# Transposing the experts' down products: fp32r products of 256 tokens, gate weights spread over the partitions by DMA, a lag of seven steps

## What is computed

```python
scores = softmax(x @ gate_w)                       # x: tokens x 128, gate_w: 128 x 8
topk_w, topk_idx = top_k(scores, 2)
topk_w = topk_w / (sum(topk_w) + 1e-20)
w_per_expert = einsum('nke,nk->ne', one_hot(topk_idx), topk_w)
for e in range(8):
    hid = silu(x @ w_gate[e]) * (x @ w_up[e])      # tokens x 256
    y = y + w_per_expert[:, e:e+1] * (hid @ w_down[e])
shared = silu(x @ ws_gate) * (x @ ws_up) @ ws_down
return x_residual + y + shared
```

## Time and profile before

| | us |
|---|---|
| median of 3 runs | 204.69 (204.68 to 205.4) |
| profiled execution | 204.75 |
| its span | 202.9 |
| TensorE busy | 191.8 (95%) |
| VectorE busy | 156.5 (77%) |
| ScalarE busy | 137.6 (68%) |
| GpSimd busy | 96.7 (48%) |

### The profile page before, as it was taken

How to read it: one execution, slowest core, us unless ns; L and a number is a source line. 1 busy time by engine, 2 the same in 40 slices (tenths; PEclk the granted TensorE clock), 3 DMA queues, 4 the chain that set the end, 5 groups by cost and what they waited for, 6 DMA issues and landing times.

```text
span 202.9 us, 4609 instructions
## 1 busy us (share of the span) xinstructions
PE 191.8 (95%) x1626; PEld 151.3 (75%) x1626; DVE 156.5 (77%) x418; ACT 137.6 (68%) x318; POOL 96.7 (48%) x145
## 2 busy tenths in 40 slices
PE   7999999899999779988999999999989999999995
PEld 7788787767877566755575657576668799999994
DVE  2579999668768695779989999999973866458744
ACT  2499878679767767289989898987976232452220
POOL 7599217688467757707739992003300017500430
PEclk9999999999999999999999999999999999999999
DMA  6980407703552015689632400000000000000001
GB/s 173 384 208 3 155 2 227 243 2 54 74 74 37 2 39 115 73 102 117 94 88 83 76 2 0 5 0 3 0 0 3 5 0 0 3 0 13 3 1 38
DMA packets 13301, 12.69 MB, mean 63 GB/s; under 512 B 1072, under 2 KB 11312, under 8 KB 13280
## 3 DMA queue, kind: packets, MB, share of 16 engines
q1 hardware_dynamic: 12176, 11.15, 25.8%
q10 hardware_dynamic: 1008, 1.06, 1.6%
q0 software_dynamic: 96, 0.20, 0.7%
HBM read 10.96 MB, written 1.44 MB: 61 GB/s over the span
## 4 chain that ended last, share of the span: by engine, by line
PE 71%; DVE 14%; ACT 8%; issue 5%; POOL 1%; DVEq 0%; ACTq 0%; POOLq 0%
PE ps L990 13%; PE ps L949 10%; PE ps L1014 8%; PE ps L926 6%; PE ps L875 6%; PE ps L759 6%; PE ps L908 5%; ACT prob L635 4%; PE ps L891 4%; PE ps L847 3%; DVE q_t L1220 3%; PE ps L731 3%; DVE low L1210 3%; PE ps L772 3%; DVE prob_t L1283 2%
## 5 line engine op out<-in xcount | busy, mean ns | idle before, releaser
L1220 DVE CUSTOM_DVE_ANT_0 q_t<-ps,mask_add 128x512 f32<-128x512 f32 x64 | 41.4, 685 | 3.4 <-PE ps L908 2.1
L509 POOL TENSOR_TENSOR prob<-prob,rec 128x512 f32<-128x512 f32 x32 | 32.7, 1047 | 22.8 <-DVE rec L1279 22.8
L635 ACT ACTIVATE prob<-ps,low 128x256 f32<-128x256 f32 x64 | 29.5, 487 | 7.4 <-DVE low L1210 7.4
L669 ACT ACTIVATE q_t<-q_t,low 128x512 f32<-128x512 f32 x44 | 29.4, 718 | 4.3 <-DVE low L1220 4.1
L949 PEld LDWEIGHTS ps<-ident,q_t 128*128 128x128 f32 x176 | 19.5, 141 | 9.4 <-ACT q_t L669 3.2
L949 PE MATMUL ps<-ident,q_t 128*128 128x128 f32 x176 | 24.1, 277 | 2.4 <-ACT place_k L712 0.8
L548 POOL TENSOR_TENSOR place_k<-place_k 128x256 f32<-128x256 f32 x10 | 7.3, 733 | 38.7 <-DVE place_k L1245 38.7
L1210 DVE TENSOR_REDUCE low<-ps 128x2 f32<-128x512 f32 x32 | 20.4, 683 | 5.9 <-PE ps L847 5.8
L655 ACT ACTIVATE q_t<-ps 128x512 f32<-128x512 f32 x18 | 10.6, 599 | 21.0 <-PE ps L990 21.0
L1266 DVE TENSOR_TENSOR q_t<-q_t,ps 128x512 f32<-128x512 f32 x18 | 12.2, 684 | 11.4 <-PE ps L990 8.2
L875 PE MATMUL ps<-prob_t,v 128*64 128x256 f32 x128 | 17.3, 390 | 2.3 <-DVE prob_t L1283 2.0
(11 more groups left out here) (183 smaller groups left out, 471.9 us busy)
## 6 DMA issues: line engine op xcount, KB each, us to landing
k_stack<-k_dram SPq DMA_DIRECT2D x18, 128.0 KB
wg<-in_L_ffn_w_gate SPq DMA_DIRECT2D x1, 1024.0 KB, 5.4
wu<-in_L_ffn_w_up SPq DMA_DIRECT2D x1, 1024.0 KB, 7.9
q_stack<-q_dram SPq DMA_DIRECT2D x6, 144.0 KB
k_dram<-prob SPq DMA_DIRECT2D x1, 768.0 KB, 3.6
w_in<-in_L_attn_Wq ACTq DMA_DIRECT2D x2, 256.0 KB, 5.4
context<-in_ctx SPq DMA_DIRECT2D x1, 512.0 KB, 5.7
w_in<-in_L_attn_Wv SPq DMA_DIRECT2D x1, 512.0 KB, 7.4
```

The lines of the kernel that those rows point to most:

```text
L509: nc.gpsimd.tensor_tensor(pr, pr, rec1[:, s % 2, r, :].unsqueeze(2).to_broadcast([P, C, S]), ALU.mult).then_inc(s_norm1, 1)
L635: e = nc.scalar.activation(prob1[:, s % 3, r, c * S:(c + 1) * S], ps[:, 2 * (s % 2) + r, c * S:(c + 1) * S], ACT.Exp, bias=low1[:, s % 2, ...
L669: nc.scalar.activation(prob2[n % 3][:, c, :], score2[n % 2][:, c, :], ACT.Exp, bias=low2[:, n % 2, c:c + 1], scale=-1.0).then_inc(s_exp2, 1)
L1220: nc.vector.tensor_tensor_reduce(out=score2[n % 2][:, c, :], in0=ps[:, 2 * (n % 2) + c, :], in1=mask_add[:, c, :], scale=1.0, scalar=3e38, ...
```

## The change

- Down products are transposed: down weights stationary, 256 tokens moving, as three fp32r products for each half f. A step has 6 products of 256 columns (L1070 of the changed kernel). y then lies with features on the partitions and tokens along the columns, so the output is written as (D, B, S); the host only views it transposed.
- The down weights are split in high and low parts on GpSimd (`split_down`), 8 in cross-attention steps n = 23 to 30 and one after row 1's normalising.
- The hidden values are split as well. VectorE writes the product silu x up back into the up bank, ScalarE copies it from there as the high part (`high_of_hidden`, one silu later), and VectorE subtracts for the low part (L1331). `s_hid` is now raised by that subtraction. There are 3 up banks (2, 3 and 6) and 8 buffers of hidden parts.
- The gate weight of a token now belongs to a column. `w_e` goes to DRAM and comes back spread over the 128 partitions (`w_wide`: 128 x 2048 floats a row, [token][expert]); VectorE multiplies by every 8th of them (`wide_weight`).
- The lag is 7 steps. In row 1 the shared expert comes last. Row 0 is summed by GpSimd wholly; in row 1 GpSimd adds for k = 1 and 2, VectorE for k = 3 to 7 (L1320) and in the end (L1304). The residual x2 is added on TensorE by two products with the identity (L1066), in steps j = 0 and 17.
- The gate weights are cut in two parts of 8 and 12 instructions. Row 0's come at n = 33, around the last copy of transposed probabilities; row 1's in steps 10 and 11, and its exponential in step 9 instead of 8.

```diff
-LAG_D = 2
-BY_POOL = 5
+LAG_D = 7
+HIDS = LAG_D + 1
+U_BANKS = (2, 3, O_BANK)
+BY_POOL = 2
...
-    6: [("turn2", 1, 0), ("turned2", 1, 0)],
-    7: [("gate", 1, 0)],
-    8: [("shift", 1, 0), ("gate_exp", 1, 0)],
-    11: [("weights", 1, 0)],
+    7: [("turn2", 1, 0), ("turned2", 1, 0)],
+    8: [("gate", 1, 0)],
+    9: [("shift", 1, 0), ("gate_exp", 1, 0)],
+    10: [("weights", 1, 0)],
+    11: [("weights", 1, 1)],
...
+            for b in range(B):
+                sp.wait_ge(s_we, b + 1)
+                load(w_dram[b].rearrange("(c p) e -> p c e", p=P), w_e[:, b * C:(b + 1) * C, :], d_wdram)
+                sp.wait_ge(d_wdram, 16 * (b + 1))
+                sp.wait_ge(s_low2, C * N_CROSS)
+                load(w_wide[:, b, :], w_dram[b].rearrange("(o t) e -> o (t e)", o=1).to_broadcast([P, S * NE]), d_wwide[b])
...
+            def split_down(k):
...
+                split(wd[:, (k - 1) % (NE + 1), :, :], [wd_parts[k][:, i, :, :] for i in range(2)]
+                      ).then_inc(s_wdparts, 1)
...
+            def high_of_hidden(i):
+
+                act.wait_ge(s_prod, i + 1)
...
+                nc.scalar.copy(hid[i % HIDS][:, 0, :, :], ps[:, U_BANKS[i % 3], :].rearrange("p (f t) -> p f t", f=FC)
+                               ).then_inc(s_hidhi, 1)
...
             def silu_step(i):
                 act.wait_ge(s_g, i + 1)
                 if i >= 2:
-                    act.wait_ge(s_hid, i - 1)
+                    act.wait_ge(s_prod, i - 1)
                 nc.scalar.activation(silu[i % 2], ps[:, i % 2, :], ACT.Silu).then_inc(s_silu, 1)
+                if i >= 1:
+                    high_of_hidden(i - 1)
...
                     up(i % 2, 0).then_inc(s_g, 1)
-                    if i >= 2:
-                        pe.wait_ge(s_hid, i - 1)
-                    up(2 + i % 2, 1).then_inc(s_u, 1)
+                    if i >= 3:
+                        pe.wait_ge(s_hid, i - 2)
...
+                    up(U_BANKS[i % 3], 1).then_inc(s_u, 1)
...
+                    if e == NE:
+                        pe.wait_ge(s_x2, b + 1)
+                        for c in range(C):
+                            mm(ps[:, y_bank(j), c * P:(c + 1) * P], x2[:, b * C + c, :], ident[:, :],
+                               start=c == 0, stop=False)
+                    for f in range(FC):
+                        for part, (hi, wi) in enumerate(BIG_PARTS):
+                            last = mm(ps[:, y_bank(j), 0:S], w[:, wi, f, :], hid[j % HIDS][:, hi, f, :],
+                                      start=e != NE and f == 0 and part == 0,
+                                      stop=f == FC - 1 and part == len(BIG_PARTS) - 1)
+                    last.then_inc(s_y, 1)
...
+            def outputs(j):
...
+                if b or k >= 3:
+                    dve.wait_ge(s_acc, b * NE + (min(k - 2, BY_POOL) if b else k - 2))
+                v.tensor_tensor(y_part[k % 2], y, wide_weight(b, e), ALU.mult).then_inc(s_ypart, 1)
+                if b and k > BY_POOL:
+                    dve.wait_ge(s_ypart, j + 1)
+                    if k == BY_POOL + 1:
+                        dve.wait_ge(s_acc, NE + BY_POOL)
...
+                    v.tensor_tensor(acc[:, b, :], acc[:, b, :], y_part[k % 2], ALU.add).then_inc(s_sum, 1)
...
             def hidden_step(i):
                 if i < N_FFN:
...
-                    v.tensor_tensor(hid[i % 3], silu[i % 2].rearrange("p (f t) -> p f t", f=FC),
-                                    ps[:, 2 + i % 2, :].rearrange("p (f t) -> p f t", f=FC), ALU.mult
-                                    ).then_inc(s_hid, 1)
+                    v.tensor_tensor(bank, silu[i % 2], bank, ALU.mult).then_inc(s_prod, 1)
+                if 1 <= i <= N_FFN:
+                    dve.wait_ge(s_hidhi, i)
+                    to = hid[(i - 1) % HIDS]
+                    v.tensor_tensor(to[:, 1, :, :], ps[:, U_BANKS[(i - 1) % 3], :].rearrange("p (f t) -> p f t", f=FC),
+                                    to[:, 0, :, :].bitcast(F32), ALU.subtract).then_inc(s_hid, 1)
                 if i >= LAG_D:
                     outputs(i - LAG_D)
```

More of the change, by code:

```diff
@@ L78 @@
     N_SELF + 32: [("gate_exp", 0, 0)],
+    N_SELF + 33: [("weights", 0, 0)],
 }
@@ L121, with expert, y_bank @@
 QSETS = ((0, 4), (4, H2))
-def y_bank(j, c):
-    return O_BANK if j == N_FFN - 1 and c == C - 1 else 4 + j % 2
+def expert(i):
+    b, k = divmod(i, NE + 1)
+    return (k - 1) % (NE + 1) if b == 0 else k
+def y_bank(j):
+    return 4 + j % 2
 def cycle(g):
@@ L391, in _ @@
                     load(wd[:, NE, :, :], a["L0_ffn_ws_down"].rearrange("(f r) n -> r f n", r=P), d_wd)
[L392 to L396, removed]
+            for b in range(B):
[4 more added lines that the diff above has]
+                load(w_wide[:, b, :], w_dram[b].rearrange("(o t) e -> o (t e)", o=1).to_broadcast([P, S * NE]), d_wwide[b])
+            sp.wait_ge(s_acc, NE)
+            load(out[:, 0, :], acc[:, 0, :], d_out)
+            sp.wait_ge(s_yout, 1)
+            load(out[:, 1, 0:P], y_out[:, 1, 0:P], d_out)
+            sp.wait_ge(d_out, 16 * 3)
         @block.gpsimd
@@ L536, in _ @@
                     split_weights(n - SPLIT_N)
[L537 to L539 removed]
+                elif 0 <= n - SPLIT_N - 2 * (NE + 1) < NE:
+                    split_down(n - SPLIT_N - 2 * (NE + 1))
+            for i in range(FFN_EARLY, N_FFN + LAG_D):
+                for kind, row, _ in FFN_BETWEEN.get(i, ()):
                     if kind == "turned2":
                         split_tokens(row)
[L542 to L551 removed]
+                    elif kind == "residual2":
+                        normalise(3 + row, x2, row * C)
+                        split_down(NE)
+                b, k = divmod(i - LAG_D, NE + 1)
+                if (b == 0 and k >= 1) or (b == 1 and 1 <= k <= BY_POOL):
+                    pool.wait_ge(s_ypart, (NE + 1) * b + k + 1)
+                    if k > 1:
+                        pool.wait_ge(s_acc, b * NE + k - 1)
+                    nc.gpsimd.tensor_tensor(acc[:, b, :], acc[:, b, :], y_part[k % 2], ALU.add).then_inc(s_acc, 1)
         @block.scalar
@@ L718, in _ @@
                 silu_step(i)
[L719 to L723, removed]
+            high_of_hidden(N_FFN - 1)
+            act.wait_ge(s_yout, 2)
+            act.dma_start(out[:, 1, P:S], y_out[:, 1, P:S]).then_inc(d_out, 16)
         @block.tensor
@@ L978, in expert_step @@
                     b, k = divmod(i, NE + 1)
-                    e, rows = (k - 1) % (NE + 1), slice(b * S, (b + 1) * S)
+                    e = expert(i)
                     if i >= 2:
@@ L1195, in first_largest @@
                     link(v.tensor_tensor(to, pick[:, cs, :], wide(4, b), ALU.is_equal))
-                first_largest(gate_s[:, cs, :], pick1[:, cs, :])
+                if part == 0:
+                    dve.wait_ge(s_gexp, b + 1)
+                    link(v.tensor_reduce(col[:, 1, cs], gate_e[:, cs, :], AX.X, ALU.add))
+                    link(v.reciprocal(col[:, 2, cs], col[:, 1, cs]))
+                    link(v.tensor_tensor(gate_s[:, cs, :], gate_e[:, cs, :], wide(2, b), ALU.mult))
+                    first_largest(gate_s[:, cs, :], pick1[:, cs, :])
+                    return
                 link(v.scalar_tensor_tensor(out=rest[:, cs, :], in0=pick1[:, cs, :], scalar=-2.0,
@@ new lines, in outputs @@
+            def outputs(j):
+                b, k = divmod(j, NE + 1)
+                e, y = expert(j), ps[:, y_bank(j), 0:S]
+                dve.wait_ge(s_y, j + 1)
+                if j == 0:
+                    v.tensor_copy(acc[:, 0, :], y).then_inc(s_ypart, 1)
+                    return
+                if e == NE:
+                    dve.wait_ge(s_sum, NE - 1 - BY_POOL)
+                    for c in range(C):
+                        t = slice(c * P, (c + 1) * P)
+                        v.tensor_tensor(y_out[:, b, t], y[:, t], acc[:, b, t], ALU.add).then_inc(s_yout, 1)
+                    return
+                if e == 0:
+                    dve.wait_ge(d_wwide[b], 16)
+                if k == 0:
+                    v.tensor_tensor(acc[:, b, :], y, wide_weight(b, e), ALU.mult).then_inc(s_ypart, 1)
+                    return
+                if b or k >= 3:
[3 more added lines that the diff above has]
+                    dve.wait_ge(s_ypart, j + 1)
@@ L1331, in _ @@
                                           ps[:, PT_BANK, :].rearrange("p (k t) -> p k t", k=2)).then_inc(s_pt2a, 1)
+                for what in AFTER_COPY.get(g, ()):
+                    between(what)
                 if n in O_READY:
```

99 lines of the change are left out of this document (45 added, 54 removed).

## The result

The changed kernel takes **211.16 us** (median of 6 runs, 210.42 to 212.57) against 204.9 (6 runs on the same chip, 204.57 to 205.4): ratio 1.031, 95% interval [1.028, 1.033], slower. The direction was forecast, the size was not: +1.4 forecast, +6.3 measured, outside the range. Three of the six executions, 211.16, 211.35 and 212.57, had a mean granted clock of 0.992; the other three, at 1.000, have a median of 210.87. The profiled execution took 210.87 with a span of 208.3 and a clock of 1.00.

A forecast was written before the change was run, and what follows sets the result against it. TensorE, gap-free in the expert stage, bounds the kernel. The up's end comes 3.1 us earlier at 194.5, including a 3.1 us stall; a 7.8 us tail ends at 202.3 against 200.9: 204.75 + 1.4 = 206.2 us, range 204.6 to 208.6.

The forecast's parts named there:

- A: Expert stage from step 0's first gate and up products to the down product behind step 9's up; forecast 19.7 us.
- The tail: Eight down steps behind the last up, VectorE's additions 0.80 us a step; end 7.8 us after the up's end.
- The stall: TensorE waits 3.1 us in all at ups 12, 13 and 14, behind row 1's gate weights on VectorE.
- B: From A's end to the down product behind step 17's up, holding the stall; forecast 20.1 us.
- C: From B's end to VectorE's last end, the tail; forecast 7.9 us.
- the chain: VectorE and ScalarE work from step 9's up to low part 11, which frees up 14's bank; 13.0 us.
- Rival 1: VectorE catches up unnoticed by TensorE, the 3.1 us of waits do not arise; 203.1 us, chance 0.12.
- Rival 2: Row 1's spread weights come late by DMA: at 7.9 us for 1 MB, 2.5 late, 208.1 us; chance 0.12.
- Rival 3: Multiplies reading weights 32 bytes apart take twice the time (0.61 us), in stall and tail; 208.6 us, chance 0.10.
- the rule cited there: Trainium skill: full SBUF speed needs at least two hits on a 16-byte line, so every strided read pays; no figure.

The follow-up runs named there:

- steps: Changed kernel with expert e reading the spread weights at a step of e + 1 floats (1 to 8), one run; multiply 0.64 us at step 8, no kernel time given.
- fourth bank: Changed kernel with four up banks instead of three from step 12 on; 210.81 us, ratio 1.027.
- ScalarE's copies: Changed kernel with ScalarE copying each expert's 256 weights into contiguous buffers before VectorE multiplies, results unchanged; 208.20 us, ratio 1.018.

## Why the prediction was wrong

**What held.** The down products run in groups of 0.71 us, and A came out 0.2 long (19.7 forecast); 0.14 of that is the pair of identity products, 0.36 us in the timeline (169.58 to 169.94) where the sum had 0.22. The tail's pair takes 0.43, behind VectorE. The copy-back into PSUM costs nothing, product and low part are as costed. The stall is at ups 12, 13 and 14, and the tail is VectorE's. Once the two costs below are gone, B and C stand at 20.2 and 8.1, 0.1 and 0.2 off. In that run step 9's up ends at 174.36 and up 14 starts 12.96 us later, where the chain link by link gave 13.0:

```profile
187.32 0.39 PE L1040 MATMUL ps<-own_parts,w_in_parts 128*128 128x256 f32 x1 [1.47 <-DVE after_keys L1331]
```

Rival 1 fell with it. Rival 2 is false: 1 MB of spread weights landed in 4.6 us, and row 1's, issued at 190.07, were thus there 1.9 us before output 9 began at 196.58:

```profile
w_wide<-w_dram SPq DMA_DIRECT2D x2, 1024.0 KB, 4.6
```

**The step that failed: "The multiply by the spread weights reads one tensor from PSUM as before; 0.34"**, with 0.61 as the upper bound. The next instruction starts 0.56 later, inside the bounds, but the sum took the lower one; the multiply is 0.64 long. Rival 3 was what happened. It was given 0.10, since no row had such a read; but the only evidence on the matter, the rule cited there, spoke against the change, and the row that I took (one PSUM, one contiguous input) did not bear on the step at all. It cost 1.8 us of stage, 0.7 in the stall and 1.1 in the tail. Rival 3 had put it at 2.4: it took 0.27 more for each, where 0.22 was measured, on outputs 3 and 4 alone, though output 2 stands in the same chain, and on all seven of the tail.

**A cost that was not in the sum:** VectorE beside GpSimd. The sum has the twenty gate instructions at the 4.12 us that they took before, and nothing for GpSimd. Three instructions of the chain (a logit and two gate instructions) stood still behind its additions, 1.1 us, and the stall passed it on whole. The trace of before showed it. The earlier trace rows are two instructions with two SBUF inputs, GpSimd idle; the same line four us later, merged, then the second of the two by itself, then GpSimd:

```profile
11.51 3.49 DVE L1113 SCALAR_TENSOR_TENSOR qk_parts<-w_in,qk_parts 128x512 fp32r<-128x512 f32 x2 [1.63 <-ACT qk_parts L581]
```

```profile
12.12 2.88 DVE L1113 SCALAR_TENSOR_TENSOR qk_parts<-w_in,qk_parts 128x512 fp32r<-128x512 f32 x1
```

```profile
11.63 2.83 POOL L442 TENSOR_TENSOR v_parts<-w_in,v_parts 128x1024 fp32r<-128x1024 f32 x1
```

The first began 0.12 us before GpSimd's subtraction and took its usual 0.69; the second began within it and took 2.88, to 0.54 past its end. I used the idle case for the tail, where GpSimd is idle, and never asked what GpSimd does during the gate block, which the change puts right behind the output that wakes it.

**The balance.** Over the forecast of 206.2 by 4.7, from the profiled execution of 210.87: strided reads 1.8; contention 1.2; the rest of A, B and C 0.5; start-up 0.5, which varies; time outside the span 0.7 (2.57 against 1.85). The median of 211.16 stands 0.3 above that execution because half of the executions had the lower mean clock. The time outside the span belongs to the change: its versions had 1.85 to 2.57 us over all executions, mostly near 1.95 or 2.4, the kernel before 1.76 to 1.86. The sum took 1.85 for it without a reason. The output goes out in another shape, but what causes it was not tried and stays open.

**Why nothing was gained at all.** A down step did shrink from 0.89 to 0.71 us, so TensorE saved the 3.2 us forecast for that, and lost 0.8 instead of 0.44 to the identity products. But VectorE's work in the stage rose by 12.0 us to 38.5, with a serial block in the middle and a tail of 8 steps that hide nothing. The version without slow reads on VectorE, contention and row 1's gate block only reaches the old time.

## What to carry to other kernels

When a change moves data into another layout, look at the step of every operand that reads it, and price a stepped read as its own form rather than by the nearest contiguous row. When TensorE's share shrinks, add up the next engine's work together with its serial blocks; what hid behind TensorE then shows whole. Before counting small VectorE instructions with two SBUF inputs at their usual length, see whether GpSimd runs a two-input operation beside them. A new order can take them out of each other's way without taking work away; here contention was worth 1.1 us of such a stretch.

## What the runs showed of the hardware

- The multiply's length by step (0.41 to 0.64 for 256 floats), and ScalarE's copy at a step of 8 floats, 0.70 instead of 0.37.
- VectorE's small instructions with two SBUF inputs began 0.23 or 0.24 us after a GpSimd addition of 0.73 us and ended 0.02 to 0.04 us after it (0.53 instead of 0.17 us); one-input reductions beside the same additions kept their 0.17. One of 512 columns that began 0.49 us after a GpSimd subtraction of 2.83 us took 2.88 instead of 0.69.
- TensorE's granted clock fell to 0.50, the 1.2 GHz level, in three of the profiled executions, after the long wait (steps, fourth bank, ScalarE's copies). The table by stage of the fourth bank (columns as above):

```profile
188.00:190.00 2.00, 0.58 (x4) 0.61 (x5) 2.00 (x5) 1.17 (x3) 0.64 (x1) 0.92 0.07 4
190.00:192.00 2.00, 2.00 (x11) 2.00 (x11) 2.00 (x4) 0.51 (x1) 0.81 (x2) 0.50 0.97 299
192.00:194.00 2.00, 2.00 (x15) 2.00 (x15) 1.31 (x3) 1.07 (x2) 0.74 (x1) 0.73 0.55 225
```

The changed kernel's profiled execution had the same wait of 2.06 us and stayed at 1.00. Three of its other five executions had a mean clock of 0.992, and so had one of the kernel before (206.13). So the wait alone doesn't decide it. What does is open. Profiled executions can thus stand over their median: ScalarE's copies took 209.75 where its other runs took 208.04 to 208.34.
